# Normalised rows of x: through a scratch in device memory instead of blocks with norm factors spread by TensorE

## What is computed

```python
x = x + xattn(layernorm(x), ctx, ctx, weights, attn_bias, mask)     # x: 8 x 512 x 512
x = x + ffn(layernorm(x), weight_q, weight_scale, ffn_bias)

def xattn(q, k, v, w, bias, drop_mask):
    attn = softmax(q @ k.T / 0.72) * drop_mask
    return (attn @ v + bias) @ w
def ffn(x, weight_q, weight_scale, bias):        # per row: symmetric int8
    x_scale = max(amax(|x|), 1e-6) / 127
    x_q = round(x / x_scale)
    return (x_q @ weight_q.T) * x_scale * weight_scale + bias
```

## Time and profile before

| | us |
|---|---|
| median of 3 runs | 341.82 (341.76 to 342.12) |
| the profiled execution, its own time | 341.56 |
| span of its profile | 339.7 |
| busy: PE, DVE, POOL, ACT | 327.8, 308.1, 237.0, 228.6 |
| granted clock of TensorE, mean | 0.995 |

### The profile page before, as it was taken

The page is one execution under the profiler, slowest core; times in us unless marked ns, Lnnn a source line. Parts: engine busy times, 40 slices in busy tenths (PEclk is TensorE's granted clock), DMA queues, the critical chain, the costliest instruction groups (busy, mean ns, idle before and its releaser), DMA issues.

```text
span 339.7 us, 6086 instructions
## 1 busy us (share of the span) xinstructions
PE 327.8 (96%) x1590; PEld 261.6 (77%) x1590; DVE 308.1 (91%) x630; ACT 228.6 (67%) x457; POOL 237.0 (70%) x368
## 2 busy tenths in 40 slices
PE   7989899999999999999999999999999999999992
PEld 6868677787787788777778887777878887787781
DVE  3687889999999999999999999999999999999887
ACT  4455786766667776667778766667776666777651
POOL 5163757778777777877777787877777877767642
PEclk9999999999999999999999999999999999999998
DMA  7949654445655545556654455565454556400002
GB/s 209 304 111 239 129 140 110 123 127 156 138 172 154 130 150 128 156 138 170 168 129 136 135 157 134 160 170 145 131 139 141 145 148 170 139 33 31 31 33 94
DMA packets 62370, 47.14 MB, mean 139 GB/s; under 512 B 17937, under 2 KB 48913, under 8 KB 62353
## 3 DMA queue, kind: packets, MB, share of 16 engines
q1 hardware_dynamic: 62352, 46.94, 51.4%
HBM read 35.13 MB, written 8.39 MB: 128 GB/s over the span
## 4 chain that ended last, share of the span: by engine, by line
PE 70%; DVE 9%; issue 1%; ACT 1%; DMA 1%; DVEq 0%; SPq 0%
PE ps_attn L511 7%; PE ps_scores L511 7%; PE ps_scores L513 7%; PE ps_scores L512 7%; PE ps_attn L513 7%; PE ps_attn L512 7%; PE ps_ffn L685 7%; PE ps_vw L511 6%; PE ps_vw L512 6%; PE ps_vw L513 6%; PE ps_pt L503 3%; DVE ffn_out L961 1%; DVE abs_max L974 1%; DMA xq_t<-x_int 1%; PE ps_xt L608 1%
## 5 line engine op out<-in xcount | busy, mean ns | idle before, releaser
L1217 POOL TENSOR_TENSOR ct_lo<-ct_raw,ct_hi 128x512 fp32r<-128x512 f32 x28 | 36.4, 1298 | 26.2 <-ACT ct_hi L742 26.2
L764 ACT ACTIVATE x_norm<-x_blocks,norm_spread 128x128 f32<-128x128 f32 x124 | 51.2, 483 | 2.3 <-ACT norm_spread L757 1.6
L511 PE MATMUL ps_attn<-vw_hi,pt_hi 128*128 128x512 f32 x124 | 51.4, 415 | 0.1
L511 PE MATMUL ps_vw<-w_hi,ct_hi 128*128 128x512 f32 x116 | 50.7, 437 | 0.0
L511 PE MATMUL ps_scores<-ct_hi,xt_hi 128*128 128x512 f32 x124 | 48.8, 394 | 0.0
L513 PE MATMUL ps_scores<-ct_hi,xt_lo 128*128 128x512 f32 x124 | 48.5, 391 | 0.0
L512 PE MATMUL ps_scores<-ct_lo,xt_hi 128*128 128x512 f32 x124 | 48.4, 391 | 0.0
L513 PE MATMUL ps_attn<-vw_hi,pt_lo 128*128 128x512 f32 x124 | 48.4, 390 | 0.0
L860 ACT ACTIVATE x_neg<-x,meanvar 128x512 f32<-128x512 f32 x31 | 22.5, 725 | 38.4 <-DVE meanvar L1132 38.4
L512 PE MATMUL ps_attn<-vw_lo,pt_hi 128*128 128x512 f32 x124 | 48.3, 389 | 0.0
L1169 POOL TENSOR_TENSOR scaled<-meanvar,scale 128x2 f32<-128x2 f32 x32 | 16.6, 519 | 42.5 <-DVE meanvar L924 42.5
(11 more groups left out here) (170 smaller groups left out, 776.2 us busy)
## 6 DMA issues: line engine op xcount, KB each, us to landing
x_in<-in_x_dram SPq DMA_DIRECT2D x32, 256.0 KB, 3.1
mask_in<-in_mask_BxSxS_fk_dram SPq DMA_DIRECT2D x32, 256.0 KB, 3.8
out_dram<-out_tile SPq DMA_DIRECT2D x31, 256.0 KB, 2.2
x_blocks<-in_x_dram SPq DMA_DIRECT2D x60, 128.0 KB, 3.5
ctx_in<-in_ctx_dram SPq DMA_DIRECT2D x56, 128.0 KB, 2.8
ctx_in<-in_ctx_dram SPq DMA_DIRECT2D x4, 256.0 KB, 4.5
x_blocks<-in_L_xattn_weights_dram SPq DMA_DIRECT2D x4, 256.0 KB, 6.6
xq_t<-x_int SPq DMA_TRANSPOSE x26, 2.4
```

The costliest lines, as they stand in the source:

```text
L511: nc.tensor.matmul(bank_, lhs_hi(t), rhs_hi(t), start=(t == 0), stop=False)
L764: last = nc.scalar.activation(x_norm[:, k, a * P:(a + 1) * P], x_blocks[:, slot(n, 4), a * P:(a + 1) * P], ACT.Identity, bias=norm1_spread ...
L1217: nc.gpsimd.tensor_tensor(ct_lo[:, batch_of(n), :, j * P:(j + 1) * P], ct_raw[:, slot(n, 2), :, :], ct_hi[:, batch_of(n), :, j * P:(j + 1) ...
```

## The change

Tiles of x are no longer loaded a second time in blocks. ScalarE normalises `x_in`, which lies in rows, with the norm factors of its own partitions in one operation of 128x512. SP stores the result to `norm_rows`, a tensor in device memory, waits until it is stored, and reads it back into `x_blocks` with the blocks moved, in four DMAs of one tile (before: four DMAs of two tiles). VectorE transposes `x_blocks` directly. The mask operation, the matmul, the copy and the four normalising operations of each tile are gone, with the constants `own_block` and `same_lane`. `normalise` of the loop is now for tile d+3, not d+2, and stands behind `pt_hi`, not ahead of it.

```diff
+            def bounce_rows(base, n, row):
+                wait_count(sp, x_norm_ready, base, n + 1)
+                rows = norm_rows[bass.ds(row, P), :]
+                sp.dma_start(rows, x_norm[:, slot(n, 2), :]).then_inc(norm_rows_stored, 16)
+                wait_rows(sp, norm_rows_stored, base, n)
+                wait_count(sp, xt_raw_ready, base, n - 4)
+                quads = rows.rearrange("(a i) d -> i a d", i=BLOCK)
+                for b in range(QUADS):
+                    blocks = x_blocks[b * BLOCK:(b + 1) * BLOCK, slot(n, 4), :]
+                    sp.dma_start(blocks.rearrange("i (a c) -> i a c", a=QUADS),
+                                 quads[:, :, b * P:(b + 1) * P]).then_inc(x_blocks_loaded[slot(n, 2)], 16)
...
             sp.wait_ge(bias_terms_ready, NT)
-            load_blocks(x_blocks, x_rows, 1 * P, 1, 1, x_blocks_loaded)
-            load_blocks(x_blocks, x_rows, 2 * P, 2, 2, x_blocks_loaded)
+            bounce_rows(0, 1, 1 * P)
...
-                n = d + 3
-                if n % 2 == 0 and exists(base, n):
-
-                    wait_count(sp, x_norm_ready, base, n - 4 + 2)
-                    load_blocks(x_blocks, x_rows, row + n * P, n, 2, x_blocks_loaded)
...
                     load_mask(row + n * P, slot(n, 4))
                 if is_tile(base, d, 0):
                     load_ffn_constants()
+                n = d + 2
+                if exists(base, n):
+                    bounce_rows(base, n, row + n * P)
                 if exists(base, d - 2) and not last_batch(base):
...
-                elif exists(base, d + 2):
-                    spread_norm(d + 2)
...
             def normalise(base, n):
...
-                for a in range(QUADS):
-                    last = nc.scalar.activation(x_norm[:, k, a * P:(a + 1) * P],
-                                                x_blocks[:, slot(n, 4), a * P:(a + 1) * P], ACT.Identity,
-                                                bias=norm1_spread[:, k, a, 1:2],
-                                                scale=norm1_spread[:, k, a, 0:1])
-                last.then_inc(x_norm_ready, 1)
+                k = slot(n, 4)
+                wait_count(act, norm1_ready, base, n + 1)
+
+                wait_rows(act, norm_rows_stored, base, n - 2)
+                nc.scalar.activation(x_norm[:, slot(n, 2), :], x_in[:, slot(n, 8), :], ACT.Identity,
+                                     bias=norm1[:, k, 1:2], scale=norm1[:, k, 0:1]).then_inc(x_norm_ready, 1)
...
-                if exists(base, d + 2):
-                    normalise(base, d + 2)
                 if exists(base, d):
...
                     nc.scalar.activation(flat(pt_hi[:, slot(d, 2), :, :]), ps_pt[:, :],
                                          ACT.Copy).then_inc(pt_hi_ready, 1)
+                if exists(base, d + 3):
+                    normalise(base, d + 3)
...
-                wait_count(dve, x_norm_ready, base, n + 1)
+                wait_blocks(dve, x_blocks_loaded, base, n)
```

More of the change, by code:

```diff
@@ L65 @@
 TAIL_STEPS = PER_BATCH + 2
-FILLS = 8
+FILLS = 7
 WARM_UPS = 7
@@ L114, in wait_dma, with wait_pair, wait_blocks, wait_rows @@
     eng.wait_ge(sems[slot(n, ring)], base * (16 // ring) + (16 * uses - PHASE * (16 // ring)))
-def wait_pair(eng, sems, base, n, skipped=0):
-    uses = (PHASE + n) // 4 + 1 - skipped
+def wait_pair(eng, sems, base, n):
+    uses = (PHASE + n) // 4
     eng.wait_ge(sems[slot(n, 4) // 2], base * (4 * QUADS) + (16 * uses - 4 * PHASE) * QUADS)
+def wait_blocks(eng, sems, base, n):
+    eng.wait_ge(sems[slot(n, 2)], base * (8 * QUADS) + 8 * QUADS * (n + n % 2))
+def wait_rows(eng, sem, base, n):
+    if isinstance(base, int):
+        if base + n > 0:
+            eng.wait_ge(sem, 16 * (base + n))
+    else:
+        assert LOOP_FIRST + n > 0
+        eng.wait_ge(sem, base * 16 + 16 * n)
 def run_steps(eng, step, tail_steps=TAIL_STEPS):
@@ L142, in xattn_ffn_kernel @@
     out_rows = out.rearrange("b s d -> (b s) d")
+    norm_rows = nc.dram_tensor("norm_rows", [TILES * P, D], F32, kind="Internal").ap()
     with ExitStack() as stack:
@@ L784, in _ @@
                 if t == 1:
-                    normalise_first()
+                    normalise(HEAD, PER_BATCH)
                 if t == PER_BATCH // 2:
@@ L793, in _ @@
                 nc.scalar.activation(w_hi[:, t, :], w_raw[:, t, :], ACT.Copy).then_inc(w_hi_ready, 1)
+            normalise(HEAD, PER_BATCH + 1)
             def step(base, d):
@@ L885, in turn_x @@
             def turn_x(base, n):
-                wait_count(dve, x_norm_ready, base, n + 1)
+                wait_blocks(dve, x_blocks_loaded, base, n)
                 wait_count(dve, xt_lo_ready, base, n - 1)
-                turn_blocks(xt_raw[:, slot(n, 2), :, :], x_norm[:, slot(n, 2), :], xt_raw_ready)
+                turn_blocks(xt_raw[:, slot(n, 2), :, :], x_blocks[:, slot(n, 4), :], xt_raw_ready)
             def turn_blocks(into, blocks, ready):
@@ L904, in turn_ctx @@
             def turn_ctx(base, n):
-                wait_pair(dve, ctx_loaded, base, n, skipped=1)
+                wait_pair(dve, ctx_loaded, base, n)
                 wait_count(dve, ct_lo_ready, base, n - 1)
@@ L924, in x_mean_var @@
                 nc.vector.bn_aggr(meanvar1[:, slot(n, 4), :], stats1[:, slot(n, 4), :]).then_inc(meanvar1_ready, 1)
-            nc.vector.memset(own_block[:, :, :], 0.0).then_inc(own_block_ready, 1)
-            dve.wait_ge(own_block_ready, 1)
-            for a in range(QUADS):
-                nc.vector.memset(own_block[a * BLOCK:(a + 1) * BLOCK, a, :], 1.0).then_inc(own_block_ready, 1)
             x_statistics(HEAD, PER_BATCH)
@@ L1179, in norm_factors @@
                                         ALU.mult).then_inc(norm1_ready, 1)
-                if is_tile(base, n, 0):
-                    return
-                wait_count(pool, norm1_ready, base, n + 1)
-                wait_count(pool, spread_done, base, n - 2)
-                nc.gpsimd.tensor_tensor(norm1_masked[:, slot(n, 2), :, :],
-                                        norm1[:, k, :].rearrange("p (a c) -> p a c", a=1).to_broadcast([P, QUADS, 2]),
-                                        own_block[:, :, :], ALU.mult).then_inc(norm1_masked_ready, 1)
-            norm_factors(HEAD, PER_BATCH)
-            for a in range(1 - QUADS, QUADS):
-                nc.gpsimd.affine_select(out=same_lane[:, :], in_=same_lane[:, :], compare_op=ALU.not_equal, fill=1.0,
-                                        base=a * BLOCK, pattern=[[-1, P]],
-                                        channel_multiplier=1).then_inc(same_lane_ready, 1)
-                pool.wait_ge(same_lane_ready, a + QUADS)
-            pool.wait_ge(own_block_ready, 1 + QUADS)
+            norm_factors(HEAD, PER_BATCH)
             for t in range(1, 3):
```

39 lines of the change are left out of this document (4 added, 35 removed).

## The result

The changed kernel takes **355.41 us** (median of four, 352.98 to 357.16), against 341.79 (341.08 to 342.12) for the kernel before on the same chip: a ratio of 1.0374, 95% interval 1.0336 to 1.0411. The forecast was 351.8, range 342.0 to 362.0, slower. The profiled execution took 357.16 us with a span of 355.4. It is the highest of the four, so two more profiles of the same kernel are used beside it: e4_after_again (352.72 us, span 350.9) and e11_after_third (356.95 us, span 355.2).

What follows compares the result with a forecast made beforehand. TensorE's list was taken to bound the kernel at 9.81 us a loop step, VectorE and the DMA transpose close behind. 341.56 + 6.4 (loop) + 4.3 (head) - 0.5 (tail) = 351.8 us, range 342.0 to 362.0.

Steps and rivals of the forecast that it cites:

- The mechanism: SP's queue in the loop: store, wait and four reads ahead of the DMA transpose make it late; a pair of steps +0.53 us.
- The sum of a round, 17.49 + s: SP's loop chain from store through reads, transpose and feed-forward spans two steps: 17.49 us plus the store's landing time.
- The gain that is left on the table: Loop without the small matmul: VectorE's 9.66 us a step comes next after TensorE's 9.81, so at most 3.6 us.
- The loop, forecast +6.4 us: The 24 loop steps: a pair takes 20.15 us against 19.62, 0.53 more for each of 12 pairs.
- how large s is: Landing time of SP's store in the loop: 2.65 us behind the context burst, 2.2 in the other steps.
- The bound of 3.4: Upper bound of the store's landing time in the loop: 3.4 us everywhere gives pairs of 20.89, +15.2 us.
- The bound of 1.7: Lower bound of the store's landing time in the loop: 1.7 us everywhere makes VectorE the bound, -3.6 us.
- the faster rival: SP's store and reads stay hidden in the loop, VectorE's 9.66 us sets the pace: 338.3 us, chance 0.12.
- The clock, a rival with 0.15: TensorE idles ahead of the head's first feed-forward and its clock falls to 1.2 GHz: about +1.8, 353.6 us, chance 0.15.
- The head, forecast +4.3: Four rounds of store, wait and reads precede the first transpose; feed-forward starts 5.7 us later, less about 1.4 slack: +4.3 us.
- ScalarE, costed at 0: ScalarE's moved normalising ends 0.24 us before `x_neg` starts; fewer operations on ScalarE and GpSimd also cost nothing: 0 us.
- The other signs: Wrong in kind if others wait for ScalarE's normalising, or VectorE waits for `x_blocks`; no size given.

Runs made afterwards that it cites:

- e4_after_again: The changed kernel run once more, unchanged: 352.72 us.
- e11_after_third: The changed kernel run again, unchanged, on another chip: 355.01, 355.51 and 356.95 us, the last one profiled; ratio to before 1.0366.
- e2: The changed kernel with blocks read from x itself, so SP need not wait for the store, which is still made: 339.25 us, ratio 0.9899.
- e1: The changed kernel with SP's wait for the store and its four block reads moved behind the DMA transpose: 344.60 us, ratio 1.0049.
- e3: The kernel before without the small spread matmul, GpSimd's mask operation and ScalarE's copy (normalising partly wrong): 338.93 us, ratio 0.9888.
- e12: The changed kernel with blocks read from x itself and the store of normalised rows left out as well: 338.42 us, ratio 0.9862.

## Why the prediction came out as it did

- **The mechanism was right.** SP's wait for its own store, ahead of the transpose, is the cost: e2 takes the wait away and e1 moves it, and the loss of 3.7% becomes a gain of 1.0% or a loss of 0.5%. The sum of a round, 17.49 + s, held as well: of the 33 rounds behind a burst in the loops of the three profiles, 29 end within 0.25 us of it. Of the other four two have the slow clock, one a late transpose (all three are told under e11), and one is 0.4 longer.
- **The gain that is left on the table** was right as a ceiling and too high as a value: VectorE's 9.66 us a step is about the floor, but the two ends of the difference were read too far apart. 9.81 is the longer of two steps by turns (9.81 and 9.78), and the 20 ordinary steps average 9.79 before and 9.70 in e3; four steps of 9.96 to 10.45 stand in both alike. That leaves 1.9 of the 3.6 us in e3 and 2.2 in e2.
- **The loop, forecast +6.4 us:** +6.3 in e4, +11.4 in the first profile, +9.6 in e11. The pair of steps was forecast at 20.15; the three profiles give 20.21, 20.64 and 20.48. The term that was mis-sized is s, "how large s is". Over all steps its mean was right: 2.43 forecast (2.65 and 2.2 by turns), 2.39 to 2.48 measured (from the issue of the store to that of the first read). But in the prediction's own sum only the stores behind a burst set the pace, since the round of the others (19.69) is shorter than the pair. These average 2.86, 2.75 and 2.76 in the first profile, e4 and e11, where 2.65 was forecast; most of the others need 2.04 to 2.12. In the first profile the eleven rounds make 2.3 us of that, and the slow clock behind the store of 5.22 adds 2.7: 6.4 + 2.3 + 2.7 = 11.4, as measured. In e11 it is 1.2 for the stores, 1.2 for the late transpose and 1.5 for the clock: 10.3, measured 9.6. In e4 the stores give 7.5, measured 6.3; that its loop meets the forecast to 0.1 us is in part luck.
- **The spread of s** was missing. Behind a burst it is anything from 2.05 to 3.8, and one store each in two of three profiles takes 4.1 and 5.2. The bound of 3.4 was thus no bound for a single store. Part of the spread was in the prediction's own equations, a = 7.83 + s and the next s = 13.14 - a: two burst stores in a row then add up to 5.31, and nothing draws them to 2.65. From 150.23 on, those of the first profile are 3.52, 2.34, 3.54, 2.21, 2.91, 2.06, 2.97 and 2.12, and neighbours add up to 5.0 to 5.9. This is worked out afterwards; no run tests it.
- **The bound of 1.7 was misread.** Of the stores in the earlier trace rows two are not of the kind named there: 128 KB each (`out_dram<-ct_raw`, at 336.7 and 337.6), landing after 1.7. The output stores of 256 KB took 2.01 to 3.39, so the faster rival's "stores land in 1.7" had no row behind it.
- **The clock, a rival with 0.15,** happened in part, and beside the forecast case, not in its place. It fell where I had placed it, ahead of the first feed-forward, in two of three profiles, and cost 1.6 us (forecast 1.8). I had not thought of it in the loop, where a late store lets TensorE idle for 3.38 and 2.14 us: there it cost 2.7 and 1.5 us. The idle time of before that left the clock at full was 1.61 us (34.62 to 36.23), not the 1.4 that a window of 34 to 36 shows. The rule of the Trainium skill that I had weighed ("TensorE: Matmul & The Clock Gate", "Part 1: The HAM clock gate": half clock when idle, back with sustained work) agrees with these rows in direction.
- **The head, forecast +4.3:** +3.4, +5.5 and +5.1. The rounds of SP were close: the transpose was forecast for 49.4 and left at 48.83, the first matmuls were forecast for 51.8 and ran at 51.47. The higher two hold the fall of the clock at the first feed-forward.
- **The tail, forecast -0.5:** -0.4 to -0.5.
- **ScalarE, costed at 0,** is not where anyone waits long: VectorE's wait for `x_neg` stays at 6.6 us in sum, before 5.9. Its slack of 0.24 us was enough. The copy and the mask operations were free, as said.
- **The other signs:** x_blocks is waited for 1.5 us in sum by VectorE, which is nothing.

The median is 3.6 us above the forecast. The loop (up to 5.0 us over its forecast, with its late transfers and slow clock), the slow clock in the head (1.6 us) and a start that was 1.2 us later than in the profile of before in two of three profiles each cover a part; the three vary from execution to execution, and I can't split the 3.6 further.

## What to carry to other kernels

A queue that issues in order turns a wait for one transfer into a delay of everything behind it; put a round trip through device memory behind the issue that somebody is waiting for, then see what is queued behind the round trip (here the context loads), and spread bursts. Work out the chain as a loop, and ask which of its transfers set the pace: the mean that counts is theirs, and what one late transfer does to the next round is part of the sum. And the time freed on the busiest engine is worth only its distance to the second.

## What the runs showed of the hardware

- A store of 256 KB out of SBUF, with a free queue, had landed 2.03 to 2.14 us after its issue, with few exceptions; behind a burst of 1 MB after 2.05 to 4.1; once after 5.2. The Trainium skill's fit for GpSimd's path ("DMA: Bandwidth & Descriptors", "Anatomy of one DMA") gives 2.6 us for 256 KB, an estimate weighed in the prediction; it is above what SP's queue shows when it is free.
- The granted clock fell to 1.2 GHz after idle times of TensorE of 2.0 us (e4, near 36), 2.1, 2.4 and 2.5 (e11), and 2.5, 3.1 and 3.4, and was back at 2.4 GHz some 4 to 6 us after the idle time. The length of one idle time doesn't decide it alone: in e11 one of 2.78 us, from 92.8 to 95.6, left the clock at 1.00, and so did 1.61 near 36 before; in e2 it was at half from 26.1 on, behind two idle times of 0.98 and 1.31 close together, while two of 1.20 and 1.31 in the first profile left it at full, and so did one of 2.11 near 50 there.
- The 8 MB of added stores in a busy queue cost nothing measurable as long as nobody waited for them (e2, e12).
